# A Mamba-2 style mixer with a LoRA feed-forward layer on one core: the chunk loads begun by another engine, one small matmul moved, and VectorE's work reordered

## What is computed

```
proj = x @ in_proj_w.T                    # gate | hs | B | C | dt
hs, B, C = silu(causal conv, 4 taps, per channel)
dt = clip(softplus(dt + dt_bias)); per chunk of 128 tokens, per head (128 heads of 64 channels, 8 groups):
  Y_diag = (C B^T * exp(segment sums) , lower triangle) @ (hs*dt)
  state  = decayed sum over chunks;  Y_off = C @ state * exp(cumsum)
y = (Y_diag + Y_off + hs*D) * silu(gate)
out = y * rsqrt(mean over the group's 1024 channels of y^2 + eps) * norm_w @ out_proj_w.T
x = layernorm(x + out);  x = layernorm(x + x @ W.T + bias + LoRA(x))
```

## Time and profile before

| | |
|---|---|
| median of 3 executions | 1777.6 us (1776.5 to 1781.23) |
| the profiled execution's own time | 1778.26 us |
| its span, first to last instruction | 1776.4 us |
| mean granted clock of TensorE | 0.976 of 2.4 GHz |
| busy: PE, DVE, ACT, POOL | 1654.8, 1349.2, 1232.6, 1010.2 us |
| one group in the loop (group 3 to group 4, same step) | 206.8 us (725.92 to 932.67) |

### The profile page before, as it was taken

One profiled execution on the slowest core, in us unless ns is written; L12 is line 12 of the kernel. 1 busy time (PEld: TensorE's weight loads), 2 busy tenths in 40 slices (PEclk: granted clock), 3 DMA queues, 4 the chain that ended last, 5 costly groups with the idle time before them and its releaser, 6 DMA issues. The chain is left out here.

```text
span 1776.4 us, 29827 instructions
## 1 busy us (share of the span) xinstructions
PE 1654.8 (93%) x9056; PEld 1300.6 (73%) x9056; DVE 1349.2 (76%) x1864; ACT 1232.6 (69%) x2383; POOL 1010.2 (57%) x815
## 2 busy tenths in 40 slices
PE   6669999899989999899999999899998999989798
PEld 5547778677767788677877777677776777777665
DVE  5466598766978689775988779776897669786676
ACT  4477767777767777677667767677776787677642
POOL 2145666565655666656566565565656665565564
PEclk9879999999999999999999999999999999999999
DMA  3644444435344333454344444454445443443421
GB/s 104 113 134 114 102 102 96 111 97 120 76 99 115 101 102 92 105 112 103 94 108 102 100 112 85 100 112 99 102 89 110 108 116 89 101 107 96 113 48 42
DMA packets 237243, 179.03 MB, mean 101 GB/s; under 512 B 17296, under 2 KB 199568, under 8 KB 236688
## 3 DMA queue, kind: packets, MB, share of 16 engines
q10 hardware_dynamic: 188736, 92.53, 25.7%
q1 hardware_dynamic: 48336, 84.40, 16.1%
HBM read 172.17 MB, written 4.72 MB: 100 GB/s over the span
## 5 line engine op out<-in xcount | busy, mean ns | idle before, releaser
L483 PE MATMUL proj<-x_hi,w_hi 128*128 128x512 f32 x1160 | 473.2, 408 | 38.4 <-POOL w_lo L923 23.5
L923 POOL TENSOR_TENSOR w_lo<-raw,w_hi 128x512 fp32r<-128x512 f32 x209 | 284.8, 1364 | 335.5 <-ACT w_hi L675 334.8
L484 PE MATMUL proj<-x_lo,w_hi 128*128 128x512 f32 x1160 | 458.6, 395 | 0.0
L485 PE MATMUL proj<-x_hi,w_lo 128*128 128x512 f32 x1160 | 458.2, 395 | 0.0
L1061 DVE SCALAR_TENSOR_TENSOR hs<-proj,uch,hs 128x511 f32<-128x511 f32 (+2 forms) x384 | 285.7, 744 | 117.8 <-ACT hs L700 112.8
L755 ACT ACTIVATE decay<-decay,tok 128x128 f32<-128x128 f32 x1024 | 313.0, 391 | 64.1 <-DMA decay<-acum_d 63.8
L962 POOL TENSOR_TENSOR dh<-dh,eac 128x512 f32<-128x512 f32 x96 | 125.7, 1310 | 348.6 <-DVE eac L1206 348.5
L483 PEld LDWEIGHTS proj<-x_hi,w_hi 128*128 128x128 f32 x1160 | 223.1, 192 | 87.1 <-issue 38.7
L1083 DVE TENSOR_TENSOR decay<-decay,cb 128x1024 f32<-128x1024 f32 x128 | 183.7, 1435 | 111.5 <-ACT decay L761 105.3
L485 PEld LDWEIGHTS proj<-x_hi,w_lo 128*128 128x128 f32 x1160 | 221.5, 191 | 48.1
L484 PEld LDWEIGHTS proj<-x_lo,w_hi 128*128 128x128 f32 x1160 | 222.6, 192 | 41.7
(11 more groups left out here) (113 smaller groups left out, 2787.4 us busy)
## 6 DMA issues: line engine op xcount, KB each, us to landing
decay<-acum_d ACTq DMA_DIRECT2D x125, 512.0 KB, 8.6
raw<-w_t SPq DMA_DIRECT2D x209, 256.0 KB, 2.7
eac<-eacum_d ACTq DMA_DIRECT2D x190, 128.0 KB, 8.4
wo_raw<-wo_t SPq DMA_DIRECT2D x32, 256.0 KB, 4.9
c_new<-wo_t SPq DMA_DIRECT2D x32, 256.0 KB, 6.5
hs<-x_t SPq DMA_DIRECT2D x4, 512.0 KB, 6.5
acc<-x_tok SPq DMA_DIRECT2D x1, 2048.0 KB, 10.2
out<-acc SPq DMA_DIRECT2D x8, 256.0 KB, 2.0
```

The source lines that it names most:

```text
L483: nc.tensor.matmul(dst[:], w_hi[:, ws, k, :], x_hi[:, k, cols], start=(k == 0), stop=False)
L484: nc.tensor.matmul(dst[:], w_hi[:, ws, k, :], x_lo[:, k, cols], start=False, stop=False)
L485: mm = nc.tensor.matmul(dst[:], w_lo[:, ws, k, :], x_hi[:, k, cols], start=False, stop=(k == KC - 1))
L923: nc.gpsimd.tensor_tensor(w_lo[:, s].rearrange("p a b -> p (a b)"), raw[:, s, :], w_hi[:, s].rearrange("p a b -> p (a b)").bitcast(F32), A ...
```

## The change

Five edits, made together:

- All loads of the chunks and units move from ScalarE's stream to SP's. In each step SP begins `decay` and `eac`, at c = 7 `uch` ahead of `tok` and `elast`, at (0,4) `gch`, and then the weights of the projection tile four tiles ahead.
- L538 leaves `project_out`; as `norm_sum` it stands two steps later, behind the first projection of the step and ahead of L623. VectorE takes its result (`take_var`) right behind `y` of that later step.
- VectorE scales `eac` for step c+1 at the end of step c, behind `g_lo`, where step c has a single tile; elsewhere it stays at the start of c+1.
- The first two `wo_lo` parts move from the start of a c = 1 step to the end of the c = 0 step; ScalarE's first two `wo_hi` parts move ahead of the drains and SiLUs of the c = 0 step.
- The feed-forward loads of the last group are begun inside SP's body, at (1,1).

```diff
 # SP
+            load_tile(0, LOOP_TILES[2], False)
+            load_tile(0, LOOP_TILES[3], False)
...
-                        for t in STEP_TILES[e][c]:
-                            first = isinstance(g, int) and g == 0 and t.n < 2
-                            if t in tiles_of(e, c, last) and not first:
-                                load_w(g, t)
...
+                        od, ed, cd = ahead(e, c, 2 if c % 2 else 4)
+                        if not (last and od):
+                            load_decay(sp, g + od, ed, cd)
+                        o2, e2, c2 = ahead(e, c, 2)
+                        if c2 % CPB and not (last and o2):
+                            load_eac(sp, g + o2, e2, c2)
+                        if c == 7 and not last:
+                            load_channels(sp, 2 * g + (e + 2), e)
+                            load_unit(sp, 2 * g + (e + 2), e)
+                        if e == 0 and c == 4 and not last:
+                            load_group(sp, g + 1)
+                        for t in tiles_of(e, c, last):
+                            off, n = divmod(t.n + 4, GRP_TILES)
+                            if not (last and off):
+                                load_tile(g + off, LOOP_TILES[n], last)
 # PE, body
+                        if e == 1 and c > 1:
+                            norm_sum(g, c - 2, last)
+                        elif e == 0 and c < 2 and not (isinstance(g, int) and g == 0):
+                            norm_sum(g - 1, 6 + c, False)
                         pe.wait_ge(xdt_ready, s + 1)
                         pe.wait_ge(mix_ready, s + 1)
 # ACT: the loads above removed, and
+                        if c == 0:
+                            wo_split_hi(g, e, (0, 1))
                         for i, t in enumerate(tiles[1:], 1):
 # DVE, body
-                        if c % CPB:
+                        if c % CPB and len(STEP_TILES[e][c - 1]) > 1:
+                            scale_off(g, e, c)
...
-                        if c == 1:
-                            wo_split_lo(g, e, (0, 1))
...
                         nc.vector.tensor_tensor(y[:], p_yd[:], dh[:], ALU.add).then_inc(y_ready, 1)
+                        if e == 1 and c > 1:
+                            take_var(g, c - 2)
+                        elif e == 0 and c < 2 and not (isinstance(g, int) and g == 0):
+                            take_var(g - 1, 6 + c)
...
                         # behind g_lo
+                        if c < 7 and (c + 1) % CPB and len(STEP_TILES[e][c]) == 1:
+                            scale_off(g, e, c + 1)
...
                         # at the end of the step, behind add_out
+                        if c == 0:
+                            wo_split_lo(g, e, (0, 1))
```

More of the change, by code:

```diff
@@ L435, in _, with load_tile @@
             load_eac(sp, 0, 0, 1)
+            def load_tile(g, t, last):
+                if last and t.e == 1 and t.kind != "G1":
+                    return
+                load_w(g, t)
+                if t.n in WO_LOADS:
+                    off, we, js = WO_LOADS[t.n]
+                    if not (last and off):
+                        for j in js:
+                            load_wo(g + off, we, j)
+            load_tile(0, LOOP_TILES[2], False)
+            load_tile(0, LOOP_TILES[3], False)
             sp.wait_ge(toks_stored, 16)
@@ new lines, in body @@
+                        if last and (e, c) == (1, 1):
+                            sp.wait_ge(gated, step(GROUPS - 1, 1, 0))
+                            for dst, src in ((ffn_w_sb, ffn_w), (lora_a_sb, lora_a), (lora_b_sb, lora_b),
+                                             (bias_sb, bass.AP(tensor=ffn_bias.tensor, offset=0, ap=[[0, P], [1, HID]])),
+                                             (lw[:], lora_w)):
+                                sp.dma_start(dst, src).then_inc(ffn_loaded, 16)
@@ L507, in front, with project_out @@
                     nc.tensor.transpose(p_misc[:, P:2 * P], bT[:, cols], ident[:]).then_inc(cb_ready, 1)
-            def project_out(g, e, c, last=False):
+            def project_out(g, e, c):
                 s = step(g, e, c)
@@ L533, in project_out, with norm_sum @@
                 mm.then_inc(out_ready, 1)
[L534 to L538, removed]
+            def norm_sum(g, c, last):
+                pe.wait_ge(sqs_ready, step(g, 1, c) + 1)
+                pe.wait_ge(cb_taken, 8 * g + (8 if c < 6 or last else c + 3))
+                wait(pe, var_taken, 8 * g + c)
+                nc.tensor.matmul(p_misc[:, 2 * P:2 * P + 1], sqs[:, c, :], ones[:], start=True, stop=True).then_inc(var_ready, 1)
             def to_tokens(n, src):
@@ L643, in body @@
                         if c:
-                            project_out(g, e, c - 1, last)
+                            project_out(g, e, c - 1)
+                            if last and (e, c) == (1, 7):
+                                norm_sum(g, 6, True)
                         elif e:
@@ L1291, in body @@
                             add_out(g - 1, 7)
+                        if last and (e, c) == (1, 7):
+                            take_var(g, 6)
+                        if c == 0:
+                            wo_split_lo(g, e, (0, 1))
                         if ffn_step and c >= 4:
```

30 lines of the change are left out of this document (10 added, 20 removed).

## The result

The changed kernel took 1785.6 us (1773.0 to 1792.5, 20 runs) against 1778.7 us (1776.0 to 1782.6, 20 runs) of the kernel before: a ratio of 1.0032, interval 1.0016 to 1.0047. The forecast was 1755 us. The profiled execution took 1789.8 us for a span of 1788.0 us, 11.6 more than before, at a mean granted clock of 0.968 (before 0.976). It is one of the longer ones: the 20 executions run from 1773.0 us at a mean granted clock of 0.977 to 1792.5 at 0.966, so sums over its steps stand about 4 us above the median.

A forecast was written before the change was run, and what follows sets the result against it. TensorE, busy 93% of the span, was taken as the bound, with only its own waits to win. Terms -19.6 + 8 - 7.5 + 1.5 - 5 = -22.6 us from 1777.6 gave 1755 us, range 1735 to 1775.

The forecast's parts named there:

- the term for (1,7): Step (1,7): L506 waits for var, 1.9 us lost in groups 0 and 6, half in five others: +8 us (4 to 13).
- (0,0) and (0,1): First steps of groups 1 to 7: earlier uch gains 3.4 us, less 0.6 for clock; -19.6 us in all (-10 to -26).
- `eac` at (0,5) and (1,5): Steps (0,5) and (1,5): scaling eac a step earlier removes L629's waits there, -7.5 us (-4 to -8).
- half 1: Steps (1,0) and (1,1): eac behind two wo_lo loses 7.7 us, waits at (1,0) give about 6; +1.5 us (-2 to +6).
- The end: Last group: earlier decay load and eac of (1,3) and (1,5) shorten it, -5 us (-1 to -9).
- The queue: Rival: with all loads in SP's order, weights land late, costing 3.7 us a group; 1785 us, chance 0.10.
- The edge: Rival: at the edge between groups SP is held up and uch lands no earlier; 1775 us, chance 0.12.
- The clock: Rival: new waits of 1.9, 3.1 and 1.6 us each bring 1.7 us low clock; 1787 at worst, 1771 at half, chance 0.08.
- two of the rivals: Slow-queue rival at 1785 us, chance 0.10, and low-clock rival at 1787 us at worst, chance 0.08 for 1771 and above.

The follow-up runs named there:

- the best version with the hold: Changed kernel, var before y, old wo order, uch at once on its own semaphore, SP's other (1,7) loads held until y is squared: 0.9848 of the kernel before.
- the best version: Changed kernel with var taken ahead of y and the wo parts in their old order, loads not held: 1754.9 us, 0.9856 of the kernel before.
- loads alone: Kernel before with only the chunk and unit loads moved to SP: 1770.8 us, 0.9952 of the kernel before.
- loads alone, only uch early: Kernel before with loads on SP; at (1,7) uch begins at once, all other loads wait until y is squared: 0.9892 of the kernel before.
- loads alone, uch and decay early: Kernel before with loads on SP; at (1,7) uch and decay begin at once, the rest wait until y is squared: 0.9894 of the kernel before.
- loads alone, all but decay and weights early: Kernel before with loads on SP; at (1,7) uch, tok, elast, eac begin at once, decay and weights wait until y is squared: 0.9891 of the kernel before.
- the change, only uch early: Changed kernel; at (1,7) SP begins uch at once and holds its other loads until y is squared: 0.9889 of the kernel before.
- the order alone: Kernel before with only VectorE's and ScalarE's new order (eac scaling, wo parts): 1790.4 us, 1.0061 of the kernel before.

## Why the prediction was wrong

**The step that failed** is the wait at the jump in the term for (1,7): "if what ends it was begun before L506, the 1.9 vanish in it", and otherwise it stays. I had taken the 1.74 us at 927.00 as given and asked only whether it hides something. It depends on the transfers that run meanwhile. In the kernel before, ScalarE began its six DMAs late, so that TensorE was through its jump before most of them ran; SP begins them from 1.3 us behind L649 on, and they run when TensorE jumps. I priced that earliness as a gain only. Of the 40.0 us at (1,7), 12 are the wait for `var` (1.7 to 1.8 in seven groups, close to the 1.9 computed, but not absorbed). 26 more belong to the five jumps: 15 are longer waits (23.0 against 7.9), and 11 are low clock behind them. At the edge shown, five triples of matmuls take 6.24 us that take 3.4 at full pace, 2.8 more; at the five it is 1.5 to 3.0. The term was off by 32 us, 26 of them at the jump; between the sum of the forecast, -22.6, and the profiled execution, +12.2, lie 35, and between the medians 31.

By the Trainium skill (Runtime: NRT & Kernel Launch, Instruction fetch mechanics) a taken branch to instructions outside the small window that an engine holds makes it fetch them by a DMA before it goes on. The trace agrees. It has transfers of kind `instruction`; on queue q8 they are 84 packets of 16 KB, and one of them comes in at each of the five jumps, in each of the twenty kernels. It ends 1.5 to 2.1 us before TensorE's first matmul behind the jump, whether TensorE waits long or not at all. From the DMA view of 923 to 924 us of the kernel before, 931 to 932 of the changed one, and 919 to 920 of the best version with the hold:

```profile
q8 instruction: 1, 0.02, 9.9%
...
q8 instruction: 1, 0.02, 7.8%
...
q8 instruction: 1, 0.02, 8.3%
```

Narrower windows place their starts at 923.64, 931.30 and 919.61. What moves with the loads is when this packet starts, reckoned from the moment at which TensorE's next matmul would be due (0.23 us behind the start of the last one):

| | packet starts, five jumps | between starts |
|---|---|---|
| the kernel before | 0.6 to 1.6 us ahead | 1.6 to 2.4 us |
| the change | 0.6 to 2.5 behind | 4.0 to 6.1 |
| loads alone | 1.2 to 3.9 behind | 4.5 to 7.2 |
| loads alone, only uch early | 1.3 to 2.0 ahead | 1.1 to 1.7 |
| loads alone, uch and decay early | 1.4 to 2.7 behind | 4.3 to 5.8 |
| loads alone, all but decay and weights early | 0.5 to 1.2 behind | 3.5 to 4.4 |
| the change, only uch early | 3.0 ahead | 0.2 to 0.5 |

The weights for the projection behind the jump were split long before it: at the edge from group 3 to 4 of the changed kernel, `w_hi` of that tile was through at 922.57 and `w_lo` at 924.29, and TensorE went on at 934.40. So the wait is for the packet, and the packet starts late when other transfers are under way. That q8 is TensorE's is read from this timing, and the moment at which the packet is asked for isn't in the trace. By the Trainium skill (DMA: Bandwidth & Descriptors, Queues, rings and completion order) each DMA engine serves its queues in turn, a packet at a time; no run here shows that by itself.

**(0,0) and (0,1), mis-sized.** The mechanism was right at each point: `uch` in time, `y` 1.14 us behind L649 in six of the seven groups, the moved norm sum without a wait, L525 waiting 3.57 us (forecast 3.1). From L649 of (0,0) to `y` of (0,1) takes 14.6 us in each of the groups 1 to 7, forecast 13.9; the two `wo_lo` take 3.19 us and not 2.4. But the way from there to the next L649 was costed as unchanged, and took 13.2 to 15.9 us, 0.9 more on average, since behind L525's wait the clock is 0.50. For the clock I had taken off 0.6 a group; with the slower `wo_lo` it is 0.7 + 0.9 = 1.6, which leaves 1.8 of the 2.8.

**`eac` at (0,5) and (1,5): the number right, the cause mostly not.** The forecast was -7.5 and -8.8 came, but the order that was to bring it gives 1.9 us alone, and the loads alone 7.3. At (0,5) TensorE still waits 4.1 us for `eac` with the order alone (4.9 before) and not at all with the loads alone: with ScalarE's DMA issues gone the wait goes too.

**Right:** half 1 (-0.2, forecast +1.5), and its parts too: in groups 0 to 6, (1,1) lost 5.5 us (forecast 7.7) and (1,0) gave 5.8 (forecast 6). The order alone costs 12.4 at (1,1) there, and the loads give 3.3 of it back, which the forecast didn't have. The end came to -3.2 (forecast -5).

**Slips in the working.** Half of 1.9 us in five groups and all of it in two is 8.6, not 8; +7.7 and -6 make +1.7, not +1.5; ScalarE begins six DMAs at the edge, not seven. None of them changes the forecast by more than 1 us.

**The rivals.** The queue did not get too slow: loads of weights land after 5.9 us instead of 2.7, but (0,7), (1,0) and (1,6) are no longer than before. The edge did not stay late. The clock took back about 11 us at (1,7), about what its rival allowed for there (seven times 1.7), but not behind the wait that it named: behind 1.69 us for `var` the matmuls start at full pace, 0.23 us apart, and the clock fell behind the lengthened wait at the jump. It was no cause of its own. That the measured 1785.6 us is close to what two of the rivals give, 1785 and 1787, is chance.

**Open** is why, with the loads held, the packet comes 2.6 to 3.0 us ahead in the kernels whose norm sum has moved and 1.3 to 2.0 in those where it has not; whether an order exists in which neither TensorE's nor ScalarE's jump meets the loads; and how much of ScalarE's wait for `uch` before the change, 2.5 to 4.9 us at seven edges, two of them without a jump back, was its jump.

## What to carry to other kernels

A wait behind a loop's jump is no constant: look at which transfers run at that moment, and before loads are begun earlier, look at which engine jumps while they run. Taking the transfers away from one engine's jump helps only if they don't fall on that of the next engine in the chain; here the best version is no faster with the loads held than with the loads at once. A result that another engine waits for is read where it arrives, not behind a larger operation, and loads that are needed at different times don't share a semaphore.

## What the runs showed of the hardware

- Between the starts on either side of its jump back, TensorE took 1.1 to 1.7 us with the loads held, 0.2 to 0.5 where the norm sum had also moved, 3.5 to 4.4 with half of them under way, and 4.0 to 7.2 with `decay` or all of them. ScalarE, where the loads met its jump, waited 7.1 to 8.4, some 1.7 of it for TensorE.
- At each of TensorE's jumps a 16 KB packet of kind `instruction` on q8 ended 1.5 to 2.1 us before its next matmul. With few other transfers it started up to 3.0 us before that matmul was due, with SP's loads under way up to 3.9 us after.
- Behind waits of 4.39 and 3.57 us TensorE's granted clock was 0.50 for 5 to 6 us (windows 936 to 940 and 958 to 962). Behind the 1.74 us at the jump before it was 1.00:

```profile
927.00:931.00 4.00, 4.00 (x18) 3.29 (x19) 2.00 (x5) 0.20 (x1) 0.00 (x0) 1.00 0.62 145
```

- Waits that were already satisfied, added to SP's stream (742 of them in the trace), cost nothing that could be measured.
